# Eight-expert loop written out with one expert-number load per tile, and linear attention's q products and tail rearranged

## The chip, the core and the metric

The kernel runs on one core of a Trainium2 chip. The metric is device time in microseconds (us) for one execution. A core has TensorE (PE; its weight loads are shown as PEld), VectorE (DVE), ScalarE (ACT), GpSimd (POOL), and SyncE (SP), which here only issues transfers. Each engine works through its own list of instructions in order; semaphores order the engines among each other.

## What is computed

A chain of eight residual blocks on x of 2 x 1024 tokens with 256 features in fp32: x = x + block(layernorm(x)). The blocks are causal attention, a mixture of four experts (one for each token), a keyed sum, the four experts again, linear attention, a mixture of eight experts (two for each token, with a shared expert), causal attention, and the eight experts again. The change concerns linear attention and the two eight-expert blocks:

```python
# linear attention, 16 heads of 16; decay = exp(-pos / n)
Q = relu(x @ Wq.T + bq) * decay;  K = relu(x @ Wk.T + bk) * decay;  V = x @ Wv.T + bv
KV = einsum('bhnd,bhne->bhde', K, V);  Ksum = K.sum(axis=2)
Z = 1.0 / (einsum('bhnd,bhd->bhn', Q, Ksum)[..., None] + 1e-6)
out = (einsum('bhnd,bhde->bhne', Q, KV) * Z) @ Wo.T + bo

# eight experts, hidden 176, the two best of each token; shared expert with hidden 352
scores = softmax(x @ gate_w);  topk_w, topk_idx = top_k(scores, 2)
g = silu(x @ w_gate[e]) * (x @ w_up[e])
routed = sum over the two e of topk_w * (g @ w_down[e])
out = routed + silu(x @ sw_gate) * (x @ sw_up) @ sw_down
```

## The kernel before

The 2048 tokens are 16 tiles of 128, in four groups g of four tiles. The stages follow each other; each writes its instructions on every engine in a fixed order by hand, with semaphore waits. PSUM has eight banks of 512 fp32 columns.

**Eight experts (`TopTwo`).** Routing sorts the 4096 token copies by expert into 39 tiles of 128 rows; each tile belongs to one expert, whose number lies in `owner`. The matmuls read it into a register of TensorE's queue (`tile_owner`, `value_load`) and address the expert's weights with it. For a tile k POOL gathers its rows from DRAM (`gather`, L1418) into one of three buffers `y`; TensorE transposes them (`turn_y`, L1766), DVE copies the transposes (`set_y`, L1886), TensorE makes gate and up products (`up`, L1773), ACT the silu (L1841), DVE the product h (L1890), TensorE transposes h (`turn_h`, L1783), DVE copies it (L1899), TensorE multiplies down (`down`, L1791 and L1792), ACT copies the answer into one of three buffers `o` (`out`, L1847), and POOL scatters it to DRAM (`store`, L1422). TensorE, ACT and DVE run this by `every_tile`: three tiles written out, a loop of eleven rounds of three tiles, three tiles written out. POOL's list is written out for all 39 tiles: wait for `turn_y` of k, gather k+3, store k-2. A step of TensorE for k is `turn_y(k+2)`, `up(k+1)`, `turn_h(k)`, `down(k-1)`; `up` and `down` each load the expert number. Routing and the first group of the shared expert stand ahead of the loop, the other groups of the shared expert (L1747, L1758) behind it.

**Linear attention (`LinearAttention`).** The norm ahead of it (`LayerNorm`) adds the results of the experts on DVE (L1436), takes statistics, normalizes tile pairs (L287), and TensorE transposes the normalized tiles group by group (`turn`, L321); ACT copies the transposes to `yt` (L337). Then TensorE makes for each group two q products (L2152, banks 0 and 1; ACT's ReLU L2188) and four key and value products (L2160, banks 2 and 3), behind all groups the sums over tokens (L2169), and for each of the 16 tiles the product with the sums (L2178, bank t % 4). DVE takes each tile through four instructions: denominator (L2218), reciprocal (L2220), times decay (L2222), and product (L2224). The projection (`Project`) transposes the 16 results by groups (`turn`, L375; copies by ACT L405, and by DVE for one half of the first group, L411), multiplies (L387) into banks 0 to 3, and DVE adds to x (L417). `finished` lets the first group's `turn` go only when all 16 tiles are done.

The weights of linear attention are issued by SP (L2131) behind the loads of the experts' results.

Of the kernel before, what the change touches and what calls it, by code (L numbers as in the profile page):

```python
# [12 lines left out]
P = 128  # L13
# [9 lines left out]
RING = 3  # L23
GQ = 4
# [52 lines left out]
class Core:  # L77


    def __init__(self, nc, ctx):  # L80
# [21 lines left out]
        self.answers = nc.dram_tensor("answer_rows", [RING * P + 2 * NTOK, D], F32, kind="Internal").ap()  # L102
# [55 lines left out]
class Stage:  # L158
# [17 lines left out]
    def tile_done(self, dve, t): pass  # L176

# [51 lines left out]
class LayerNorm(Stage):  # L229
# [6 lines left out]
    def __init__(self, c, k, before):  # L236
# [11 lines left out]
        self.early_logits = None  # L248
# [83 lines left out]
    def scalar(self, act):  # L332
        c, k = self.c, self.k
        for g in range(NG):
            for f, done in enumerate((self.yt0, self.yt1)[0:2 if g < NG - 1 else 1]):
                act.wait_ge(self.turned, FT * (NG * k + g) + f + 1)
                act.activation(c.yt[:, f, 512 * g:512 * g + 512], self.bank(g, f)[:, :],  # L337
                               ACT.Copy).then_inc(done, 1)


class Project(Stage):
# [7 lines left out]
    def __init__(self, c, k, source, w, before):  # L349
        self.c, self.k, self.source, self.w, self.before = c, k, source, w, before  # L350
# [7 lines left out]
    def tensor(self, pe):  # L358
# [748 lines left out]
class Routing(Stage):  # L1107
# [12 lines left out]
    def __init__(self, c, kind, ln, experts, top, w, bias, const, carve, **more):  # L1120
# [46 lines left out]
        self.spare_rows = P if top == 1 else RING * P  # L1167
        if top == 2:
# [5 lines left out]
        ln.early_logits = self.multiply_logits  # L1174
# [3 lines left out]
            orders=e + (RING if top == 2 else 0), hits=1, before=1, owners=1, counters=4, stored=16 * NG, hot=4 * top, tile_hot=2 * top, scaled=top,  # L1178
# [32 lines left out]
    def gpsimd(self, pool):  # L1211
# [3 lines left out]
        if self.top == 2:  # L1215
            spare = self.spare.rearrange("p (i j) -> p i j", j=RING)
            for j in range(RING):
                pool.memset(spare[:, :, j:j + 1], float(P * j)).then_inc(self.orders.sem, 1)
# [169 lines left out]
    def set_rows(self, dve):  # L1388
# [6 lines left out]
        if self.top == 2:  # L1395
            dve.wait_ge(self.orders.sem, self.orders.at(self.e + RING))
            then(dve, dve.tensor_scalar(self.row_outf, rows[:, 0:tiles], float(RING - 1), float((RING - 1) * P), ALU.mult,
# [232 lines left out]
class TopTwo(Routing):  # L1630
# [6 lines left out]
    def __init__(self, c, ln, experts, weights, w, const, carve):  # L1637
# [3 lines left out]
        per_slot = 16 * (tiles // RING)  # L1641
        super().__init__(
            c, "top_two", ln, experts, 2, w, None, const, carve, y_in0=per_slot, y_in1=per_slot, y_in2=per_slot,
            y_turned=tiles, y_set=tiles, gu=tiles, silu=tiles, h_clear=RING, h_done=tiles, h_turned=tiles,
            ht_set=tiles, down=tiles, o_set=tiles, o_out0=per_slot, o_out1=per_slot, o_out2=per_slot, gathered0=32,
# [3 lines left out]
         self.h_turned, self.ht_set, self.down, self.o_set, o_out0, o_out1, o_out2, g0, g1, g2, g3, added1,  # L1649
# [872 lines left out]
```

## Time and profile before

| | us |
|---|---|
| median of 3 runs (2033.89 to 2037.41) | 2034.59 |
| the profiled execution | 2033.5 |
| its span, first to last instruction | 2031.4 |
| TensorE busy in the span | 1817.6 (89%) |
| VectorE busy | 1124.7 (55%) |
| ScalarE busy | 756.8 (37%) |
| GpSimd busy | 553.4 (27%) |
| share of TensorE in the chain of work that ended last | 73% |

The span is what the hardware profiler saw between the first and the last instruction. An engine's busy time leaves out register, branch and semaphore instructions; "issue" in a row means that an engine waited for nothing the profile shows. [...]

### The profile page before, as it was taken

How to read it: one execution, taken by the hardware profiler on the slowest of the kernel's cores; microseconds unless marked ns; L12 is line 12 of the kernel's file. 1: busy time of each engine (PE TensorE's matmuls, PEld its weight loads, DVE VectorE, ACT ScalarE, POOL GpSimd, SP SyncE). 2: the span in 40 equal slices, each digit the busy share in tenths (PEclk: the TensorE clock that was granted, in tenths of full speed). 3: DMA queues.
4: the chain of work that ended last, by engine and by line, in shares of the span. 5: the costliest groups of instructions: out<-in, count | busy, mean ns of one | idle time of the engine just before them, and what ended most of it. 6: DMA issues, size and time to landing. Idle time of an engine off the chain costs nothing.

```text
span 2031.4 us, 32807 instructions
## 1 busy us (share of the span) xinstructions
PE 1817.6 (89%) x10668; PEld 1014.0 (50%) x10673; DVE 1124.7 (55%) x2329; ACT 756.8 (37%) x1469; POOL 553.4 (27%) x950
## 2 busy tenths in 40 slices
PE   7799999998979997776999878898987999988988
PEld 4344444443446664464666536565553444455654
DVE  6688888886332222873222155733465888746334
ACT  3277777776411111112111110222132676741221
POOL 2322222222201111451111130256223222223650
PEclk9599999999789999878999979999996999998999
DMA  3311111114210002001000140122414122001223
GB/s 108 91 32 38 41 41 41 41 41 167 85 55 26 21 23 85 25 1 57 21 23 23 41 156 1 59 78 85 129 45 90 24 41 40 3 30 57 82 78 124
DMA packets 82063, 114.22 MB, mean 56 GB/s; under 512 B 17272, under 2 KB 61464, under 8 KB 81176
## 3 DMA queue, kind: packets, MB, share of 16 engines
q1 hardware_dynamic: 70808, 82.23, 14.0%
q0 software_dynamic: 11136, 30.42, 4.7%
q8 instruction: 72, 1.18, 0.2%
q14 instruction: 47, 0.39, 0.1%
HBM read 78.35 MB, written 33.69 MB: 55 GB/s over the span
## 4 chain that ended last, share of the span: by engine, by line
PE 73%; DVE 15%; issue 4%; DMA 3%; POOL 1%; ACT 1%; SPq 0%; another core or an unknown queue 0%; POOLq 0%; DVEq 0%; ACTq 0%
PE psum L1530 13%; PE psum L1057 10%; PE psum L1041 8%; PE psum L1551 6%; PE psum L1002 6%; DVE region_a L805 6%; PE psum L1773 5%; PE psum L1747 3%; PE psum L1791 2%; PE psum L1758 2%; PE psum L1792 2%; PE psum L1540 2%; PE psum L2160 1%; PE psum L931 1%; PE psum L1026 1%
## 5 line engine op out<-in xcount | busy, mean ns | idle before, releaser
L805 DVE TENSOR_REDUCE region_a<-psum 128x1 f32<-128x640 f32 (+7 forms) x576 | 528.2, 954 | 108.1 <-PE psum L1007 58.1
L909 ACT ACTIVATE region_w<-psum 128x512 f32<-128x512 f32 x864 | 465.6, 600 | 222.1 <-PE psum L1041 218.6
L1530 PE MATMUL psum<-region_w,region_a 128*128 x608 | 271.0, 599 | 1.4 <-DVE region_a L1611 1.2
L1057 PE MATMUL psum<-region_w,region_a 128*32 128x512 f32 (+3 forms) x2304 | 253.8, 514 | 1.0 <-POOL region_w L732 0.6
L732 POOL TENSOR_SCALAR_AFFINE_SELECT region_w<-region_w 128x512 f32<-128x512 f32 x192 | 121.8, 635 | 458.4 <-ACT region_w L909 454.1
L1422 POOL DMA_INDIRECT answer_rows<-region_a x116 | 114.5, 987 | 423.3 <-ACT region_a L1580 345.6
L1002 PE MATMUL psum<-region_a,y_norm 48*128 48x512 bf16 (+7 forms) x816 | 224.4, 351 | 5.0 <-DVE region_a L805 4.3
L1041 PE MATMUL psum<-y_norm,region_a 51*128 51x512 bf16 (+1 forms) x612 | 205.4, 399 | 6.1 <-DMA y_norm<-region_a 4.2
L1530 PEld LDWEIGHTS psum<-region_w,region_a 128*128 128x128 f32 x608 | 113.8, 192 | 132.0 <-issue 132.0
L1618 DVE TENSOR_TENSOR region_a<-psum,region_a 128x512 f32<-128x512 f32 x76 | 52.5, 691 | 214.9 <-PE psum L1530 214.9
L1418 POOL DMA_INDIRECT region_a<-token_rows,region_a x116 | 112.9, 973 | 146.4 <-DVE region_a L1394 86.7
L1551 PE MATMUL psum<-region_w,region_a 128*128 x608 | 137.7, 379 | 1.9 <-ACT region_a L1590 1.9
L1041 PEld LDWEIGHTS psum<-y_norm,region_a 51*128 51x128 bf16 (+1 forms) x612 | 51.0, 96 | 160.8 <-ACT region_w L909 108.6
L1773 PE MATMUL psum<-region_w,region_a 128*128 x312 | 114.2, 489 | 18.4 <-issue 17.2
L1551 PEld LDWEIGHTS psum<-region_w,region_a 128*128 128x128 f32 x608 | 112.7, 190 | 17.1 <-issue 3.3
L1585 ACT ACTIVATE region_a<-psum 128x512 f32<-128x512 f32 x76 | 45.4, 597 | 187.0 <-PE psum L1530 187.0
L1005 PE MATMUL psum<-region_a 64*128 64x128 bf16 x512 | 112.8, 226 | 0.0
L1007 PE MATMUL psum<-region_a,identb 64*128 64x64 bf16 x512 | 98.0, 194 | 0.0
L321 PE MATMUL psum<-identf,y_norm 128*128 128x128 f32 x256 | 47.5, 340 | 56.3 <-DVE y_norm L287 46.0
L1623 DVE COPY region_a<-psum 128x512 f32<-128x512 f32 x38 | 26.3, 692 | 128.0 <-PE psum L1540 128.0
L1747 PE MATMUL psum<-y_t,region_w 128*128 128x512 f32 (+1 forms) x192 | 85.7, 594 | 0.9 <-ACT region_a L1847 0.9
L1002 PEld LDWEIGHTS psum<-region_a,y_norm 48*128 48x128 bf16 (+1 forms) x816 | 65.5, 99 | 41.7 <-DVE region_a L805 21.7
(218 smaller groups left out, 2631.2 us busy)
## 6 DMA issues: line engine op xcount, KB each, us to landing
y_norm<-a_q SPq DMA_DIRECT2D x132, 64.0 KB
token_rows<-y_norm SPq DMA_DIRECT2D x16, 512.0 KB, 5.2
y_norm<-answer_rows SPq DMA_DIRECT2D x16, 512.0 KB, 6.0
y_norm<-b_q SPq DMA_DIRECT2D x36, 128.0 KB
region_w<-in_f_wg SPq DMA_DIRECT2D x1, 4096.0 KB, 13.3
region_w<-in_f_wu SPq DMA_DIRECT2D x1, 4096.0 KB, 13.5
region_w<-in_f_wd SPq DMA_DIRECT2D x1, 4096.0 KB, 14.8
region_w<-answer_rows SPq DMA_DIRECT2D x8, 512.0 KB, 7.9
```

Source lines behind the costliest of these rows:

```text
L732: pool.affine_select(p, p, pattern=[[0, GQ], [1, P]], channel_multiplier=-1, base=0, compare_op=ALU.is_ge, fill=0.0)\
L805: dve.tensor_reduce(dst, src, AX_X, ALU.max, negate=True).then_inc(self.ring_done.sem, 1)
L909: act.activation(self.p[col % P_RING][:, :, i % 4, :], c.bank[ST_BANKS[s % 3]].rearrange("p (h t) -> p h t", h=GQ), ACT.Exp, scale=self.sc ...
L1002: mm = pe.matmul(bank[:, 0:n], q, kp[lo_row:hi_row, lo:lo + n], start=True, stop=not diag, skip_group_check=True)
L1041: mm = pe.matmul(bank[:, :], self.kp[slot][0:self.srows, P * j:P * j + P], self.qp[slot][0:self.srows, :, P * i:P * i + P], start=True, st ...
L1057: mm = pe.matmul(c.bank[ACC_BANK][32 * h:32 * h + 32, P * lo:512], self.vp[slot][:, j, :], self.p[col % P_RING][:, h, lo:4, :], start=(j = ...
L1418: pool.indirect_dma_start(y, None, self.c.tokens[:, :], bass.IndirectOffsetOnAxis(ap=self.row_in[:, k:k + 1], axis=0)).then_inc(done.sem, 16)
L1422: pool.indirect_dma_start(self.c.answers[0:self.spare_rows + self.top * NTOK, :], bass.IndirectOffsetOnAxis(ap=self.row_out[:, k:k + 1], a ...
L1530: mm = pe.matmul(bank[:, :], self.yt[:, f, :], w[:, f, bass.ds(own * self.hidden + 512 * half, 512)], start=(f == 0), stop=(f == FT - 1))
L1551: mm = pe.matmul(c.bank[7][:, 0:D], self.ht[:, j, :], self.wd[:, bass.ds((own * (last + 1) + j) * D, D)], start=(j == 0), stop=(j == last))
L1747: mm = pe.matmul(c.bank[6 * (n % 2) + k][0:m, :], weight[:, f, P * j:P * j + m], c.yt[:, f, 512 * g:512 * g + 512], start=(f == 0), stop=( ...
L1773: mm = pe.matmul(self.gu_bank[j][:, 0:2 * self.hidden], self.yt[j][:, f, :], w.wgu[:, f, bass.ds(own * (2 * self.hidden), 2 * self.hidden) ...
```

## The change

In `TopTwo`, `every_tile` writes all 39 tiles out. The expert number is loaded once for each tile, behind `up` of the tile before it, and kept until `down`. There are five answer buffers instead of three, in the space of `ctx` behind the shared expert's buffers, and POOL stores three tiles behind instead of two. In linear attention, the q products of groups 0 and 1 stand ahead of the norm's transposes of groups 2 and 3, with their ReLUs behind ACT's copies of groups 1 and 2. The tail takes two tiles at a time: the denominator is the sum plus EPS / decay, which leaves out the multiplication by decay. The projection's first `turn` waits for its own four tiles; its first products wait for all 16.

TensorE's list inside the expert loop, before; L1446 is the load of the expert number, for `up` (L1773) and for `down` behind `turn_h` (L1783), and ISA and REGISTER_ALU are register instructions:

```order
L1446 ISA
L1446 TENSOR_LOAD region_a
L1446 ISA x2
L1771 REGISTER_ALU
L1773 ISA
L1773 MATMUL psum<-region_w,region_a 128x352
L1773 ISA
L1773 MATMUL psum<-region_w,region_a 128x352
L1779 REGISTER_ALU
L1783 MATMUL psum<-identf,region_a 128x128 x2
L1446 ISA
L1446 TENSOR_LOAD region_a
```

The same list now, one step; L1774 is `turn_y`, L1781 `up`, L1458 the load, L1792 `turn_h`, L1800 and L1801 `down`:

```order
L1774 MATMUL psum<-identf,region_a 128x128 x2
L1781 ISA
L1781 MATMUL psum<-region_w,region_a 128x352
L1781 ISA
L1781 MATMUL psum<-region_w,region_a 128x352
L1458 TENSOR_LOAD region_a
L1458 ISA x2
L1792 MATMUL psum<-identf,region_a 128x128 x2
L1800 ISA
L1800 MATMUL psum<-region_w,region_a 128x256
L1801 ISA
L1801 MATMUL psum<-region_w,region_a 128x256
```

One load stands in a step instead of two, behind the `up` matmuls instead of ahead of them, and none ahead of `down`.

TensorE's list from the norm into linear attention, before (L321 transposes, L2152 q products, L2160 key and value products):

```order
L321 MATMUL psum<-identf,y_norm 128x128 x32
L2152 MATMUL psum<-y_t,region_a 128x512 x4
L2160 MATMUL psum<-region_a,y_t 128x512 x8
L2152 MATMUL psum<-y_t,region_a 128x512 x4
L2160 MATMUL psum<-region_a,y_t 128x512 x8
```

The same place now (L323 transposes, L2179 q products, L2202 key and value products):

```order
L323 MATMUL psum<-identf,y_norm 128x128 x16
L2179 MATMUL psum<-y_t,region_a 128x512 x4
L323 MATMUL psum<-identf,y_norm 128x128 x8
L2179 MATMUL psum<-y_t,region_a 128x512 x4
L323 MATMUL psum<-identf,y_norm 128x128 x8
L2202 MATMUL psum<-region_a,y_t 128x512 x16
```

Two groups of q products moved between the transposes, and two groups of key and value products now follow each other.

DVE's list in the tail, before, two tiles:

```order
L2218 TENSOR_SCALAR region_a<-psum,region_a 128x16
L2220 RECIPROCAL region_a<-region_a 128x16
L2222 TENSOR_SCALAR region_a<-region_a 128x16
L2224 TENSOR_TENSOR ctx<-psum,region_a 128x256
L2218 TENSOR_SCALAR region_a<-psum,region_a 128x16
L2220 RECIPROCAL region_a<-region_a 128x16
L2222 TENSOR_SCALAR region_a<-region_a 128x16
L2224 TENSOR_TENSOR ctx<-psum,region_a 128x256
```

The same list now, four tiles:

```order
L2260 TENSOR_TENSOR region_a<-psum,region_a 128x32
L2263 RECIPROCAL region_a<-region_a 128x32
L2267 TENSOR_TENSOR ctx<-psum,region_a 128x256 x2
L2260 TENSOR_TENSOR region_a<-psum,region_a 128x32
L2263 RECIPROCAL region_a<-region_a 128x32
L2267 TENSOR_TENSOR ctx<-psum,region_a 128x256 x2
```

Two tiles have four instructions instead of eight.

The diff, cut to its core:

```diff
+O_RING = 5
...
 class LayerNorm
     def turn(self, pe, g):
-        if g == 3 and self.early_logits:
-            self.ready(pe, 1)
-            self.early_logits(pe, 0)
-            self.early_logits(pe, 1)
+        if self.early:
+            self.early.before_turn(pe, g)
...
     def scalar(self, act):
+            if self.early:
+                self.early.behind_copies(act, g)
...
 class Project
         def multiply(g):
             copied(0, g)
             copied(1, g)
+            if g == 0:
+                self.products_free(pe)
...
 class TopTwo
-    def every_tile(self, eng, step):
-        rounds = self.tiles // RING
-        for j in range(RING):
-            step(0, j, j, self.tiles - 1 - j)
-        with eng.Fori(1, rounds - 1) as i:
-            for j in range(RING):
-                step(i, j, i * RING + j, RING)
...
+    def every_tile(self, step):
+        for k in range(self.tiles):
+            step(k)
...
     def gpsimd(self, pool):
-            if k >= 2:
-                store(k - 2)
+            if k >= 3:
+                store(k - 3)
+        store(self.tiles - 3)
...
     def tensor(self, pe):
-        def up(i, j, k):
-            own = self.tile_owner(pe, k)
+        def up(k):
+            j = k % RING
...
-        def down(i, j, k):
-            own = self.tile_owner(pe, k)
+        def down(k):
+            j, own = k % RING, owner.pop(k)
...
+        def step(k):
+            if k + 2 < self.tiles:
+                turn_y(k + 2)
+            if k + 1 < self.tiles:
+                up(k + 1)
+            if k + 2 < self.tiles:
+                owner[k + 2] = self.tile_owner(pe, k + 2)
+            turn_h(k)
+            if k:
+                down(k - 1)
...
     def scalar(self, act):
+        def out(k):
+            j = k % O_RING
             act.wait_ge(self.down.sem, self.down.at(k + 1))
+            if k >= O_RING:
+                act.wait_ge(self.o_out[j].sem, self.o_out[j].at(16 * (k // O_RING)))
             act.activation(self.o[j], self.o_bank, ACT.Copy).then_inc(self.o_set.sem, 1)
...
 class LinearAttention
+    def before_turn(self, pe, g):
+        if g >= 2:
+            self.multiply_q(pe, g - 2)
+    def behind_copies(self, act, g):
+        if g in (1, 2):
+            self.relu_q(act, g - 1)
+    def multiply_q(self, pe, g):
+        c = self.c
+        if g == 0:
+            pe.wait_ge(self.w_in, self.W_IN)
+        self.ln.ready(pe, g)
...
     def vector(self, dve):
+        dve.reciprocal(self.eps, self.decay).then_inc(self.den_step, 1)
+        dve.wait_ge(self.den_step, 1)
+        dve.tensor_scalar(self.eps, self.eps, self.EPS, None, ALU.mult).then_inc(self.den_step, 1)
...
+        for n in range(NT // 2):
+            den, rden = self.den[n % 2], self.rden[n % 2]
+            both = c.psum[:, 2 * (n % 2):2 * (n % 2) + 2, 0:FT * (P + nh)].rearrange("p n (f e) -> p n f e", f=FT)
+            eps = over(self.eps[:, 2 * n % BT:2 * n % BT + 2], 2, FT * nh)
+            dve.wait_ge(self.outp, 2 * n + 2)
...
+            dve.tensor_tensor(den.rearrange("p n (f h) -> p n f h", f=FT), both[:, :, :, P:P + nh],
+                              eps.rearrange("p n (f h) -> p n f h", f=FT), ALU.add).then_inc(self.den_step, 1)
+            dve.reciprocal(rden, den).then_inc(self.den_step, 1)
+            for i in range(2):
+                t = 2 * n + i
+                dve.tensor_tensor(c.cx[:, D * t:D * t + D].rearrange("p (f h e) -> p f h e", f=FT, h=nh),
...
     def finished(self, pe, g):
-        pe.wait_ge(self.o_done, 4 * g + 4 if g else NT)
+        pe.wait_ge(self.o_done, 4 * g + 4)
+
+    def products_free(self, pe):
+        pe.wait_ge(self.o_done, NT)
```

## Rows read from the trace of the kernel before

**Rows 1.** Busy time by stage: stretch, length, engines' busy us, PEclk, DMA share, GB/s
```profile
1171.00:1188.00 17.00, 8.82 (x33) 6.02 (x34) 15.33 (x51) 3.55 (x7) 9.34 (x19) 0.50 0.27 87
...
1854.80:1976.90 122.10, 109.78 (x465) 73.19 (x465) 42.54 (x116) 27.35 (x78) 72.37 (x74) 0.99 0.25 79
```

**Rows 2.** The chain that ended last, three expert steps: start us, us, what
```profile
1380.67 0.27 issue
...
1383.87 0.58 issue
...
1390.36 1.45 PE psum L1773 x4
```

**Rows 3.** Register instructions, 1380 to 1382.5: count, ns min/median/max, first and last start
```profile
L1446 PEldq FUSED_REGOPS  x4: 46/106/151, 1380.0 to 1381.8; - x4
L1446 PEldq TENSOR_LOAD <-region_a x2: 300/302/303, 1380.1 to 1381.5; - x2
...
L1773 PEldq FUSED_REGOPS  x2: 46/46/46, 1380.8 to 1381.0; - x2
```

**Rows 4.** TensorE in order of time, expert loop: start us, us, instructions [idle before]
```profile
1322.02 1.35 PE L1773 MATMUL psum<-region_w,region_a 128*128 x4
...
1324.51 1.35 PE L1773 MATMUL psum<-region_w,region_a 128*128 x4
...
1429.86 1.36 PE L1773 MATMUL psum<-region_w,region_a 128*128 x4
...
1436.74 2.84 PE L1747 MATMUL psum<-y_t,region_w 128*128 128x512 f32 x6 [0.47 <-ACT region_a L1847]
```

**Rows 5.** POOL in order of time in the same loop
```profile
1323.97 0.97 POOL L1418 DMA_INDIRECT region_a<-token_rows,region_a  x1 [0.30 <-issue]
...
1326.54 0.97 POOL L1418 DMA_INDIRECT region_a<-token_rows,region_a  x1 [0.30 <-issue]
```

**Rows 6.** The gathers' line over the whole execution: ns min/median/max, and landing
```profile
L1418 POOL DMA_INDIRECT region_a<-token_rows,region_a x116: 941/970/1201, 573.1 to 1963.5; - x116
...
DMA to landing us min/median/max: 2.6/2.7/3.0
```

**Rows 7.** TensorE in order of time, the norm ahead of linear attention
```profile
1178.08 1.11 PE L321 MATMUL psum<-identf,y_norm 128*128 128x128 f32 x4 [1.17 <-DVE y_norm L287]
```

**Rows 8.** The line that loads linear attention's weights, its last load
```profile
L2131 SPq DMA_DIRECT2D region_a<-in_member x1: 428/428/428, 1170.1 to 1170.1; - x1
...
DMA to landing us min/median/max: 6.1/7.0/7.7
```

**Rows 9.** The chain that ended last, start of linear attention
```profile
1188.10 5.44 PE psum L2152 x8
1193.54 6.87 PE psum L2160 x16
1200.41 3.43 PE psum L2152 x8
```

**Rows 10.** DVE in order of time, tail of linear attention and the projection's copy
```profile
1239.17 0.23 DVE L2218 TENSOR_SCALAR region_a<-psum,region_a 128x16 f32<-128x16 f32 x1
1239.43 0.26 DVE L2220 RECIPROCAL region_a<-region_a 128x16 f32<-128x16 f32 x1
1239.72 0.24 DVE L2222 TENSOR_SCALAR region_a<-region_a 128x16 f32<-128x16 f32 x1
1239.99 0.42 DVE L2224 TENSOR_TENSOR ctx<-psum,region_a 128x256 f32<-128x256 f32 x1
...
1257.38 0.42 DVE L2224 TENSOR_TENSOR ctx<-psum,region_a 128x256 f32<-128x256 f32 x1
...
1259.93 0.69 DVE L411 COPY y_t<-psum 128x512 f32<-128x512 f32 x1 [2.13 <-PE psum L375]
```

**Rows 11.** TensorE in order of time, the same stretch
```profile
1241.72 0.70 PE L2178 MATMUL psum<-region_a,region_w 128*128 128x136 f32 x4 [0.46 <-DVE ctx L2224]
...
1261.32 4.79 PE L387 MATMUL psum<-region_a,y_t 128*128 128x256 f32 x16
```

More of the change, by code:

```diff
@@ L1166, in __init__ @@
         self.row_out = self.row_in
[L1167 removed]
+        self.spare_rows = P if top == 1 else O_RING * P
         if top == 2:
@@ L1641, in __init__ @@
         per_slot = 16 * (tiles // RING)
+        o_slots = {f"o_out{i}": 16 * len(range(i, tiles, O_RING)) for i in range(O_RING)}
         super().__init__(
@@ L1661, in __init__ @@
         self.sh = [r.take([512]) for _ in range(3)]
+        self.o = [r.take([D]) for _ in range(O_RING)]
         self.back = [c.yn, Carve(c.region["w"], weights.end).take([NT, D])]
@@ L1793, in down @@
                 .then_inc(self.down.sem, 1)
-        def step(i, j, k, left):
-            if left >= 2:
-                turn_y(*self.later(i, j, 2))
-            if left >= 1:
-                up(*self.later(i, j, 1))
-            turn_h(i, j, k)
-            if not (isinstance(k, int) and k == 0):
-                down(*self.later(i, j, -1))
+        def step(k):
[6 more added lines that the diff above has]
+            turn_h(k)
+            if k:
+                down(k - 1)
         assert w.shared_tiles == 3
@@ L1816, in tensor @@
         pe.wait_ge(self.s_added.sem, self.s_added.at(2))
-        for j in range(2):
-            turn_y(0, j, j)
-        up(0, 0, 0)
-        self.every_tile(pe, step)
-        down(self.tiles // RING - 1, RING - 1, self.tiles - 1)
+        for k in range(2):
+            turn_y(k)
+            owner[k] = self.tile_owner(pe, k)
+        up(0)
+        self.every_tile(step)
+        down(self.tiles - 1)
         pe.wait_ge(self.o_set.sem, self.o_set.at(self.tiles))
@@ L1859, in scalar @@
             self.scale_lanes(act, k)
-        silu(0, 0, 0)
-        self.every_tile(act, step)
-        out(self.tiles // RING - 1, RING - 1, self.tiles - 1)
+        silu(0)
+        self.every_tile(step)
+        out(self.tiles - 1)
         for n in range(m, 4 * m):
@@ L1891, in mul, with step @@
                               ALU.mult).then_inc(self.h_done.sem, 1)
-        def step(i, j, k, left):
-            if left >= 2:
-                set_y(*self.later(i, j, 2))
-            if left >= 1:
-                mul(*self.later(i, j, 1))
+        def step(k):
+            j = k % RING
+            if k + 2 < self.tiles:
+                set_y(k + 2)
+            if k + 1 < self.tiles:
+                mul(k + 1)
             dve.wait_ge(self.h_turned.sem, self.h_turned.at(k + 1))
@@ L1912, in vector @@
         dve.wait_ge(self.h_clear.sem, self.h_clear.at(RING))
-        for j in range(2):
-            set_y(0, j, j)
-        mul(0, 0, 0)
-        self.every_tile(dve, step)
+        for k in range(2):
+            set_y(k)
+        mul(0)
+        self.every_tile(step)
         pairs_behind = {5: 0, 6: 1, 7: 2, 8: 3, 10: 4, 11: 5}
```

147 lines of the change are left out of this document (76 added, 71 removed).

## The prediction

> **What bounds the kernel now.** I read the busy times by stage first, to see which of the edited places are limited by TensorE. Two are the expert loops of the two top-two stages: 122.10 us for the second, with TensorE busy 109.78 of it at a granted clock of 0.99 [rows 1]. The third is the linear attention with the norm ahead of it. In that norm, 1171 to 1188, TensorE is busy 8.82 of 17.00 us at a clock of 0.50 while DVE is busy 15.33 [rows 1]: DVE sets the pace and TensorE has room.
>
> In the loop I then read the chain of waits over three steps. One `up` begins behind a gap at 1380.67 + 0.27 = 1380.94, the third after it at 1390.36 [rows 2], so a step takes 9.42 / 3 = 3.14 us. The chain is TensorE all along, with gaps that read "issue", the largest here 0.58 us ahead of an `up` [rows 2]: TensorE has its data and waits for its own instruction queue. What sits there is the load of the expert number. Its first register instruction starts at 1380.0, the load at 1380.1 takes 300 ns, and the first register instruction of the matmul starts at 1380.8 [rows 3]: 0.8 us of queue, twice in a step, because `up` and `down` each load the number. Where the queue was ahead, a whole step took 1324.51 - 1322.02 = 2.49 us [rows 4]. So 0.65 us of each step is queue, at most 0.33 for each load, if the branch and the register arithmetic cost nothing beside them.
>
> POOL is the next limit: a gather and a store together take 1326.54 - 1323.97 = 2.57 us when neither waits [rows 5]. So the loop can fall from 3.14 to about 2.57, not below.
>
> **The change part by part. The loops.** Written out, a step loses one load, the register arithmetic and a third of a branch. The load that stays moves behind the two `up` matmuls. Their four records take 1.35 us [rows 4] and cover 0.8 us of queue, as long as the queue runs ahead of the array. I cost that load at nothing; if the cover fails it costs up to 0.33 a step. POOL's program has no loop before or after, so its instructions keep their price. It stores three tiles behind the gather now instead of two, so a store finds its answer ready, and the gather behind it starts earlier. Five answer buffers keep ACT's copy from waiting for a scatter: with 2.57 us a tile the buffer comes round after 12.9 us. A gather lands 2.7 us after its issue [rows 6] and has about three steps, 7.7 us, to do so. I see no wait added for DVE or ACT, whose queues lose their loops too.
>
> The sum for the first loop: the `up` at 1324.51 is the fifth of 39 [rows 4], so 34 follow.
> - By TensorE: 1324.51 + 34 x 2.49 = 1409.2 for the last `up`.
> - By POOL: the gather at 1323.97 is the seventh [rows 5]; with the later store the eighth stands there, and 31 remain to the last. 1323.97 + 31 x 2.57 + 2.7 for landing + one step of 2.49 = 1408.8.
>
> The two limits nearly meet, and two such limits jostle each other, so I take 1410. From the last `up` to the shared experts it is 1436.74 - 1429.86 = 6.88 us [rows 4], made of waits between engines, which I keep. The loop then ends at 1416.9 instead of 1436.74: 19.8 us. The second has the same span within 1 us, so both give 39.6 us.
>
> **The q products.** Two of four groups move between the transposes of the norm. TensorE reaches the first when the second group's transposes end, 1178.08 + 1.11 = 1179.2 [rows 7]. It then waits for the stage's weights: the last load is issued at 1170.1 and takes at the least 6.1, at the most 7.7 us to land [rows 8], so 1176.2 to 1177.8, with 1.4 us in hand. If they came later, the transposes queued behind would wait, and with them ACT's copies, but DVE's norm would not. In the kernel before, the first q group took 5.44 us and the second 3.43 [rows 9]. I take 5.44 for the first, since it again starts at the low clock, and 3.43 for the second. Between them and after come eight transposes each; four take 1.11 us at the low clock [rows 7], so eight take 1.1 at the high one. 1179.2 + 5.44 + 1.1 + 3.43 + 1.1 = 1190.3. The key and value products then start at 1190.3 instead of 1193.54, and the 3.43 us of the second q group between them are gone [rows 9]: 3.2 + 3.4 = 6.6 us. ACT's two new ReLUs stand between copies whose transposes come later in TensorE's own order, so they delay nothing.
>
> [...]
>
> **The tail.** Per tile DVE does four instructions, at 1239.17, 1239.43, 1239.72 and 1239.99; the last of sixteen such tiles has its product at 1257.38 [rows 10], so a tile takes (1257.38 - 1239.99) / 15 = 1.16 us and the product itself 1.16 - 0.82 = 0.34. A pair is now 0.26 + 0.29 + 2 x 0.34 = 1.23, eight pairs 9.8 instead of 18.5 us: 8.7 saved. I take 8.5, since two of the instructions are twice as wide. TensorE must deliver two tiles in 1.23 us; four records take 0.70 when they start from a wait [rows 11], and the second tile's start when a pair ends. That fits; at 1.40 a pair it would cost 1.4 us in all. The two small new instructions for eps over decay lie ahead of the key products' first result, beside TensorE.
>
> Then `turn` of the projection no longer waits for all sixteen tiles. Before, DVE's last product ended at 1257.38 + 0.42, its own copy came at 1259.93 [rows 10], and the first projection product at 1261.32 [rows 11]: 3.5 us. Now the transposes lie beside the last pair, and what remains is DVE's copy, 0.69 us, and its hand-over: 0.9. Saved: 2.6.
>
> Linear attention in all: 6.6 + 8.5 + 2.6 = 17.7 us. **Sum:** 39.6 + 17.7 = 57.3. The profiled execution took 2033.5 (its span 2031.4 and 2.1 around it), 1.1 under the median 2034.59. 2033.5 - 57.3 = 1976.2, so a median of about **1977**.
>
> **The rivals.**
> 1. The load that stays is not covered. For it: in the loop before, the queue does fall behind the array. Against it: one load less per step gives the queue back 0.8 us where 0.65 were missing. Price: 2.49 + 0.33 = 2.82 a step, 34 x 0.33 = 11.2 a loop, the gain 8.6: 2033.5 - 17.2 - 17.7 + 1.1 = 2000.
> 2. POOL's issues stretch when the other engines crowd beside it. A gather's issue takes 0.97 in the median and 1.20 at its longest [rows 6]. If all took 1.20, the pair would be 2.80, 31 x 0.23 = 7.1 later in each loop: 1991. Against it: beside a DVE that was busy a third of the loop the median stays at 0.97. [...]
> 3. The q products gain nothing, since the clock stays at 0.50 under them: 2 x 6.86 for products and 2 x 2.2 for transposes end at 1197.3 instead of 1190.3. That eats the 6.6 whole: 1984. Against it: the rise seen in the same products [rows 9].
> 4. Slower: the load behind `up` runs only once those matmuls have left the array. The queue's 0.8 us then stand bare in every step, with 0.2 to restart: 3.49 a step, 0.35 x 34 = 11.9 more in each loop, less the 17.7: 2033.5 + 23.8 - 17.7 + 1.1 = 2041. It decides from 0.92 us a step (0.65 + 17.7 / 68). Against it: the 0.8 us of queue from 1380.0 [rows 3] left a gap of only 0.27 in the chain [rows 2], so the load ran while earlier matmuls were in the array.
>
> **How the numbers follow.** Forecast 0.64, rivals 0.12, 0.10, 0.10 and 0.03; 0.01 for something that cancels by chance. The forecast's own ends are 1966 (tighter hand-overs at the loop's end and a warmer projection) and 1985. The range of eight in ten takes in rivals 2 and 3 and part of the way to rival 1: 1966 to 1996. A measurement here tells 0.2% (4 us) from no change. Only rival 4 is slower: faster 0.96, same 0.01, slower 0.03.
>
> **What would show it.** Steps of `up` 2.5 to 2.6 us apart, POOL nearly without idle in the loop and "issue" gone ahead of `up`; key products starting near 1190; tail pairs 1.25 us apart; the first projection product within 1 us of DVE's last. Steps near 2.8 with "issue" behind the load would mean rival 1, POOL issues above 1.1 us rival 2. I am wrong if a step stays at 3.1: then the wait was never the loads.

## The result, and the profile of the kernel after

The changed kernel takes 2007.83 us (median of 4 runs, 2005.97 to 2012.86) against 2034.24 for the kernel before on the same chip (4 runs): 0.9867 of its time, with a 95% interval of 0.9848 to 0.9885. It is faster by 26.4 us (1.3%), clear of the noise, where 57.3 us were forecast; the time is outside the range. The profiled execution took 2007.0, its span is 2005.2.

Linear attention gave about 19 us, a little more than the 17.7 forecast. The loops gave 5 each instead of 20. TensorE in order of time in the first loop (start us, us, instructions [idle before]); L1781 is `up`, L1792 `turn_h`, L1752 the shared expert behind the loop:

```profile
1296.64 2.71 PE L1781 MATMUL psum<-region_w,region_a 128*128 x4
...
1325.92 1.35 PE L1781 MATMUL psum<-region_w,region_a 128*128 x4
...
1328.40 1.35 PE L1781 MATMUL psum<-region_w,region_a 128*128 x4
...
1330.89 1.35 PE L1781 MATMUL psum<-region_w,region_a 128*128 x4
1334.23 0.41 PE L1792 MATMUL psum<-identf,region_a 128*128 128x128 f32 x2 [1.99 <-DVE region_a L1916]
...
1335.66 1.35 PE L1781 MATMUL psum<-region_w,region_a 128*128 x4
...
1407.78 1.35 PE L1781 MATMUL psum<-region_w,region_a 128*128 x4
...
1414.29 1.98 PE L1752 MATMUL psum<-y_t,region_w 128*128 128x512 f32 x4 [0.47 <-ACT ctx L1861]
```

The first `up` of the loop before, in the same view, and then the page's line for `up` in both loops, before and after (busy us, mean ns | idle ahead of it). The count is one of records: the two matmuls of `up` for each of 2 x 39 tiles, 156 in the program, stand in both traces as 312, the two transposes of `turn_y` as 156 (L1766 before, L1774 after):

```profile
1313.76 2.71 PE L1773 MATMUL psum<-region_w,region_a 128*128 x4
```
```profile
L1773 PE MATMUL psum<-region_w,region_a 128*128 x312 | 114.2, 489 | 18.4 <-issue 17.2
```
```profile
L1781 PE MATMUL psum<-region_w,region_a 128*128 x312 | 111.5, 482 | 0.3 <-DVE region_a L1901 0.2
```

Most steps are as forecast: 1328.40 - 1325.92 = 2.48 and then 2.49 us, against 3.14 before [rows 2], and the 17.2 us of "issue" ahead of `up` are gone. But the next step takes 4.77, and such a step comes about every fourth time. From the first `up` to the last it is 1407.78 - 1296.64 = 111.1 us, 2.92 for each of 38 steps; to the shared experts it is 117.7, against 1436.74 - 1313.76 = 123.0 before (the end in [rows 4]). The second loop takes 117.5 instead of 122.1 [rows 1].

The long step in the same view for ACT (L1854 is the silu, L1861 the copy of the answer) and, last row, DVE (L1916, the copy of h):

```profile
1328.39 0.39 ACT L1861 ACTIVATE ctx<-psum 128x256 f32<-128x256 f32 x1 [0.77 <-PE psum L1801]
1332.25 0.32 ACT L1854 ACTIVATE region_a<-psum 128x176 f32<-128x176 f32 x1 [3.48 <-PE psum L1781]
1333.72 0.38 ACT L1861 ACTIVATE ctx<-psum 128x256 f32<-128x256 f32 x1 [1.15 <-remote]
```
```profile
1333.66 0.43 DVE L1916 COPY region_a<-psum 128x256 f32<-128x256 f32 x1 [0.71 <-remote]
```

ACT's silu at 1332.25 needs the `up` that began at 1328.40 and ended at 1329.75 by TensorE's row. It starts 2.5 us after that, though ACT had nothing else to do and the silu waits for nothing but its `up`. "Remote" is the page's word for a releaser that it can't name: at 1333.66 and 1333.72 DVE and ACT start within 0.1 us of each other, on transposes and products of TensorE that had ended 3.7 and 2.9 us earlier. TensorE's signals come late here. Those of the others don't: `turn_h` at 1334.23 follows DVE's end at 1334.09. The lateness stands in no row of TensorE's, where `up` has its usual 1.35 us, only in the idle time of those who wait, such as ACT's 3.48 us ahead of the silu. Whether the matmul itself ended late or only its signal came late, no row tells; this text calls both a late signal.

POOL over the same stretch; L1434 is the store, L1430 the gather:

```profile
1322.27 0.99 POOL L1434 DMA_INDIRECT answer_rows<-ctx,region_a  x1 [1.63 <-ACT ctx L1861]
1323.56 0.97 POOL L1430 DMA_INDIRECT region_a<-token_rows,region_a  x1 [0.30 <-issue]
...
1331.28 0.97 POOL L1430 DMA_INDIRECT region_a<-token_rows,region_a  x1 [0.30 <-issue]
1334.38 0.99 POOL L1434 DMA_INDIRECT answer_rows<-ctx,region_a  x1 [2.12 <-ACT ctx L1861]
```

From 1322.27 to 1332.25 POOL issues eight indirect transfers without a pause, at the durations of before [rows 5]. ACT's late start at 1332.25 falls on the end of the eighth. That is a hint, not a proof; the experiments had to show which of the things in the loop makes the signals late.

### The profile page after: what moved, and what is told of

The parts are those of the page before. It is cut to its first block, busy times and chain, and to the rows that moved or that the text cites. A ratio compares the mean times of both kernels' runs of the same rounds, so it can differ in the third digit from the quotient of the medians.

```text
span 2005.2 us, 31961 instructions
## 1 busy us (share of the span) xinstructions
PE 1801.9 (90%) x10672; PEld 1012.1 (50%) x10673; DVE 1121.3 (56%) x2299; ACT 755.6 (38%) x1469; POOL 555.1 (28%) x954
## 4 chain that ended last, share of the span: by engine, by line
PE 70%; DVE 16%; issue 4%; DMA 3%; another core or an unknown queue 2%; POOL 1%; ACT 1%; SPq 0%; POOLq 0%; DVEq 0%; ACTq 0%
PE psum L1542 13%; PE psum L1064 9%; PE psum L1048 7%; DVE region_a L812 7%; PE psum L1563 7%; PE psum L1009 6%; PE psum L1781 4%; PE psum L1752 3%; PE psum L1763 2%; PE psum L1800 2%; PE psum L1552 2%; PE psum L1801 1%; PE psum L938 1%; PE psum L1033 1%
## 5 line engine op out<-in xcount | busy, mean ns | idle before, releaser
L1430 POOL DMA_INDIRECT region_a<-token_rows,region_a x116 | 113.1, 975 | 147.5 <-DVE region_a L1406 86.8
L1434 POOL DMA_INDIRECT answer_rows<-region_a x38 | 37.6, 990 | 345.5 <-ACT region_a L1592 345.5
L1781 PE MATMUL psum<-region_w,region_a 128*128 x312 | 111.5, 482 | 0.3 <-DVE region_a L1901 0.2
L1434 POOL DMA_INDIRECT answer_rows<-ctx,region_a x78 | 77.2, 990 | 66.8 <-ACT ctx L1861 49.1
L323 PE MATMUL psum<-identf,y_norm 128*128 128x128 f32 x256 | 44.7, 326 | 52.4 <-DVE y_norm L291 42.2
L1752 PE MATMUL psum<-y_t,region_w 128*128 128x512 f32 (+1 forms) x192 | 85.7, 594 | 0.9 <-ACT ctx L1861 0.9
```

Of the source, the lines that this page charges most:

```text
L1430: pool.indirect_dma_start(y, None, self.c.tokens[:, :], bass.IndirectOffsetOnAxis(ap=self.row_in[:, k:k + 1], axis=0)).then_inc(done.sem, 16)
L1434: pool.indirect_dma_start(self.c.answers[0:self.spare_rows + self.top * NTOK, :], bass.IndirectOffsetOnAxis(ap=self.row_out[:, k:k + 1], a ...
L1752: mm = pe.matmul(c.bank[6 * (n % 2) + k][0:m, :], weight[:, f, P * j:P * j + m], c.yt[:, f, 512 * g:512 * g + 512], start=(f == 0), stop=( ...
L1781: mm = pe.matmul(self.gu_bank[j][:, 0:2 * self.hidden], self.yt[j][:, f, :], w.wgu[:, f, bass.ds(owner[k] * (2 * self.hidden), 2 * self.hi ...
```

## The experiments

All of them are compared by the time from the first `up` to the last in the first loop: 116.1 us before, 111.1 after. (The expectations call this 37 steps; it is 38.) A loop of 2.49 us steps throughout takes 94.0. Traces of one and the same loop code differ by some 2 us (that of the kernel before took 116.1 us here and 113.9 in lin_only), so a smaller difference between two traces tells nothing.

### Which of three things in the loop: the load, the place in the program, or the stores

const_owner, the register load and the address arithmetic away:

```
-                owner[k + 2] = self.tile_owner(pe, k + 2)
+                owner[k + 2] = (k + 2) // 5
```

> The changed kernel, but the expert number of tile k is the constant k // 5: nothing is loaded into a register and no address is computed in the expert loops (the answers use other experts' weights, the work is the same). In the changed kernel a free step is 2.49 us, but every fourth step or so TensorE's signals to ACT and DVE come 1 to 2.8 us late, and first up to shared experts takes 117.6 us. Theory 1, the register load makes TensorE's signals late: no late signals, 39 steps of 2.49, about 103 us a loop, 1978 in all. Theory 2, the lateness comes at fixed distances in TensorE's instruction stream (about 130 recorded instructions from one to the next): with 25 or 26 instead of 33 a step it comes every fifth step instead of every fourth, some 3 us a loop, 2001. Theory 3, the gathers and stores on POOL's queue cause it: unchanged, 2007.

Measured: 2006.43 us, 109.5 from first to last `up`. Long steps remain (one of them, 1342.23 to 1346.31, in the timeline of its `up`s):

```profile
1342.23 1.45 PE L1781 MATMUL psum<-region_w,region_a 128*128 128x352 f32 x4
1346.31 1.35 PE L1781 MATMUL psum<-region_w,region_a 128*128 128x352 f32 x4
1348.80 1.35 PE L1781 MATMUL psum<-region_w,region_a 128*128 128x352 f32 x4
```

Theory 1 falls; the 1.7 us less than in after lie within the difference between traces.

pe_loop0 is the changed kernel, but TensorE alone keeps its loop, with one load a tile in a register of its own, at a chosen place of the program; before_slot only moves TensorE's loop in the kernel before. If the place in the program made the signals late, as theory 2 has it, the loop in another place would change that:

```
+        with c.nc.Fori(1, rounds - 1, engines=[pe.engine], head_slot={pe.engine: 0}) as i:
+            for j in range(RING):
+                step(i, j, i * RING + j, RING)
...
+        at = {eng.engine: 0} if eng is self.c.nc.tensor else None
+        with self.c.nc.Fori(1, rounds - 1, engines=[eng.engine], head_slot=at) as i:
```

> [...] Theory 2 (place in the instruction stream): no late signals inside the loop, steps of 2.5 to 2.6, a loop of 103 to 107 us, 1978 to 1986. Theory 1 (register load) and theory 3 (POOL's queue): late signals as in the changed kernel, 113 to 118 a loop, 2000 to 2008.

> [...] In the kernel before, one signal in each round of three tiles is about 1 us late. Theory 2: that lateness goes, a round takes 8.4 instead of 9.4 us, 11 rounds, 2 loops: 2034 - 22 = 2012. Theories 1 and 3: 2034, as before.

Measured: pe_loop0 2012.58 (4 runs, 2007.27 to 2014.28), 115.2 in the loop; before_slot 1.0015 of before (1.0004 to 1.0026). Theory 2 falls. And writing TensorE's loop out was worth little by itself: with it kept, the kernel takes 0.9874 of before (0.9848 to 0.99), which can't be told from 0.9867, though the loop in its one trace is 4 us longer than in after.

no_store, the indirect stores away:

```
-            self.scatter(pool, k, self.o[k % O_RING], self.o_out[k % O_RING])
+            pass
```

> The changed kernel without the 39 stores of answers in each expert loop (what is read back afterwards are token rows, as many bytes). Theory 3, the queue's stores make TensorE's signals late: steps of 2.49 throughout, about 103 us instead of 117.6 from the first up to the shared experts, 1978 in all. Theories 1 and 2 (register load, place in the instruction stream): the loops stay at 115 to 118 us, 2003 to 2007.

Measured: 1975.24 us, 94.0 in the loop, and every step 2.49:

```profile
1341.41 1.35 PE L1781 MATMUL psum<-region_w,region_a 128*128 x4
1343.90 1.35 PE L1781 MATMUL psum<-region_w,region_a 128*128 x4
1346.38 1.35 PE L1781 MATMUL psum<-region_w,region_a 128*128 x4
```

Theory 3 holds: the stores cost the loop 17 us. The kernel without stores comes near the 1977 us that I had forecast for the change with them.

### What of a store counts

narrow_store writes 16 numbers a row instead of 256; half_rows sends 64 of the 128 rows; no_gather keeps the stores and drops the gathers behind the third; no_store_incs has no stores, but SP raises a semaphore as often. Theory A is that the completions of the transfers crowd TensorE's signals (the kernel waits for a count of 16 for each transfer), theory B that the bytes do, theory C that POOL's indirect issues do:

```
-            self.scatter(pool, k, self.o[k % O_RING], self.o_out[k % O_RING])
+            pool.indirect_dma_start(narrow[0:self.spare_rows + self.top * NTOK, :], ...
+                                    self.o[k % O_RING][:, 0:16], None)
...
+                                    bass.IndirectOffsetOnAxis(ap=self.row_out[0:64, k:k + 1], axis=0),
+                                    self.o[k % O_RING][0:64, :], None)
...
-                self.gather(pool, k + RING, self.y[k % RING], self.y_in[k % RING])
...
+            for i in range(16):
+                sp.sem_inc(self.o_out[0].sem, 1)
```

> The changed kernel, but each store of an answer writes 64 bytes a row instead of 1024 (what is read back afterwards are token rows). The same number of issues by POOL, of rows and of completions, a sixteenth of the bytes. Without the stores the 37 steps from the second up on took 94.0 us, with them 111.1. [...] Theory B, the bytes: 94 to 96. Theory C, the number of indirect issues on POOL: stays near 111.

> The changed kernel, but each store sends 64 of the 128 rows (what is read back afterwards are token rows). If the number of rows counts, a pair needs 1.5 issues' worth, 0.75 x 2.96 = 2.22 us, under the free step: 94 to 97 us for the 37 steps. If the issue as such counts, whatever its rows: 110 to 111 us.

> The changed kernel with its stores, but without the gathers behind the first three (the later tiles use the rows that lie in the buffers). Theory A, completions: half as many, as without the stores, so 94 to 96 us for the 37 steps. Theory B, bytes of the stores: stays near 111. Theory C, indirect issues on POOL: half as many, 94 to 96.

> The kernel without stores, but for each tile SP raises a semaphore that nobody waits for 16 times, as the completions of a store do. Theory A, semaphore updates crowd TensorE's signals: late signals come back, 103 to 111 us for the 37 steps. Theories B and C: 94, no late signals.

Measured, first to last `up`: narrow_store 111.4 us, half_rows 110.6, no_gather 94.0, no_store_incs 94.3. Neither bytes nor rows count (theory B falls), nor do semaphore updates alone (theory A). Gathers alone do no harm, stores alone neither: in the loop it takes both, two indirect issues a tile. Groups of POOL's instructions in half_rows (line, count | busy us, mean ns | idle):

```profile
L1430 POOL DMA_INDIRECT region_a<-token_rows,region_a x31 | 29.8, 961 | 11.8 <-issue 9.7 <-PE psum L1776 2.1
L1701 POOL DMA_INDIRECT answer_rows<-ctx,region_a x28 | 25.6, 912 | 24.2 <-ACT ctx L1863 18.5 <-issue 5.8
```

Half the rows take 912 ns to issue instead of 990, and POOL still waits for ACT: it is not POOL that is short of time.

### Is it that POOL is busy, or that it issues

plain_store stores by plain transfers from SP's queue, pool_plain by plain transfers from POOL's; pool_busy and pool_busy4 store nothing and let POOL fill local memory two or four times a tile instead:

```
+            sp.dma_start(self.c.answers[at:at + P, :], self.o[k % O_RING])
...
+            pool.dma_start(self.c.answers[at:at + P, :], self.o[k % O_RING])
...
+            for i in range(4 * k, 4 * k + 4):
+                pool.memset(self.idle, 0.0)
```

> The changed kernel, but the answers are stored to rows in order by plain transfers on SP's queue, 128 KB each, with 16 completions each, and POOL issues the gathers alone (what is read back afterwards are token rows). Theory A, completions: late signals stay, 105 to 111 us. Theory B, bytes: near 111. Theory C, indirect issues on POOL: 94 to 96.

> The kernel without stores, but where a store stood POOL fills 128 x 256 numbers in its local memory twice, 2 x 0.57 us, about the time of a store's issue, with no transfer behind it (what is read back afterwards are token rows). Theory C-busy, a POOL that is busy all the time delays TensorE's signals: late signals, about 110 us for the 37 steps. Theory C-issue, the descriptors of the indirect transfers do it: 94 us, no late signals.

> As pool_busy, with four fills of 0.31 us for each tile instead of two: 4 x 0.31 and a gather of 0.95 are 2.2 us of POOL for each tile of 2.49, more than the 1.96 of a gather and a store. If a busy POOL delays TensorE's signals: late signals, 105 to 111 us from the first to the last up. If the indirect transfers do it: 94 us.

> The changed kernel, but POOL stores the answers with plain transfers to rows in order, on its own queue, as many as before (what is read back afterwards are token rows). If any transfer that POOL issues counts: 105 to 111 us from the first to the last up, as with indirect stores. If only indirect ones do: 94 us, as with plain stores on SP's queue.

Measured: plain_store 94.0, pool_busy 93.9, pool_busy4 94.7, pool_plain 94.1. Busy times from 1300 to 1390 (length, busy us of PE, PEld, DVE, ACT, POOL, then TensorE's granted clock as a share of full speed, DMA share, GB/s), after, pool_busy4, pool_plain, in this order:

```profile
1300.00:1390.00 90.00, 81.36 (x371) 58.28 (x370) 34.95 (x95) 20.88 (x61) 58.44 (x60) 0.98 0.27 87
```
```profile
1300.00:1390.00 90.00, 89.81 (x431) 66.87 (x431) 40.06 (x110) 25.06 (x72) 75.19 (x170) 1.00 0.18 52
```
```profile
1300.00:1390.00 90.00, 90.00 (x428) 66.79 (x427) 39.06 (x107) 24.57 (x70) 54.12 (x69) 0.99 0.32 102
```

In pool_busy4 POOL is busy 75.19 of 90 us, more than the 58.44 of after, and TensorE isn't held up: a busy POOL is harmless. (pool_busy told less: its fills took 0.31 us. The 0.57 was the mean of a group of fills of several shapes.) In pool_plain POOL issues as many transfers as in after and they move more bytes in the time, 102 against 87 GB/s: harmless too. no_store had also taken away ACT's wait for a landed store; no_gather, whose stores are indirect, keeps that wait at 94.0, so it isn't the cause. What is left is the indirect issue, two of them for each tile. A plain issue is shorter as well (587 ns in the mean in pool_plain, 990 for an indirect store in after), so whether its kind or its length counts stays open.

step_282 makes TensorE's step longer than POOL's pair, so that POOL has time to pause:

```
-            for f in range(FT):
+            for f in (0, 1, 0, 1):
```

> The changed kernel, but TensorE does more in each step: the two transposes of the gathered rows twice, and one of the two of h twice, 0.33 us more, so that a free step is 2.82 us, longer than POOL's pair of 2.57. Theory C1, POOL's two indirect issues a tile need about 2.96 us in something that they share with TensorE's signals, however they are spaced: the 37 steps stay at 110 to 111 us. Theory C2, it is that POOL issues without a pause, and any pause clears it: no late signals, steps of 2.82, 104 to 105 us, so a longer step makes a shorter loop.

Measured: 111.4 in the loop. Here are three of its `up`s:

```profile
1331.65 1.35 PE L1781 MATMUL psum<-region_w,region_a 128*128 x4
...
1334.47 1.35 PE L1781 MATMUL psum<-region_w,region_a 128*128 x4
...
1338.04 1.35 PE L1781 MATMUL psum<-region_w,region_a 128*128 x4
```

Free steps of 2.82 and then one of 3.57: 0.33 us more work in each step, and the loop is as long as without it. Theory C1 holds: the pair of indirect issues needs some 2.92 us, 1.46 for each on average. A pause doesn't clear it: in this run's trace POOL paused 0.53 to 0.55 us ahead of each of four stores, from 1305.97 to 1314.42, and behind them ACT's copy at 1317.57 still came 1.0 us after its `down` had ended (1316.53). A shorter step of TensorE only collects the difference into a rarer, longer stall.

### The two parts alone

lin_only has the linear attention of after and, with the class `TopTwo` of before, its expert loops (too long to print). before_no_store takes the stores out of the kernel before, as no_store does:

```
-            self.scatter(pool, k, self.o[k % RING], self.o_out[k % RING])
+            pass
```

> The kernel before with the linear attention's part of the change alone (q products inside the norm, tail by pairs, projection's transposes ahead); the expert loops are those of the kernel before. By the traces of before and after the first up of the first loop came 17.1 us earlier though the stage ahead of the linear attention ended 1.9 us later: 19 us from this part, 2034 - 19 = 2015. By the prediction 17.7 us: 2016.

> The kernel before without the 39 stores of answers in each expert loop (what is read back afterwards are token rows). It still loads the expert number twice a tile. If the loads in TensorE's queue made its step 3.14 us instead of 2.49, as the prediction has it, the steps stay near 3.1 and 37 of them take 115 us. If it was POOL's two indirect issues a tile, the steps fall to 2.5 to 2.7 and 37 of them take 94 to 100 us.

Measured: lin_only 2013.15 (4 runs), 0.991 of before (0.9891 to 0.993), 19.6 us less. before_no_store 2004.63, 98.6 us in the loop; its `up`s:

```profile
1361.83 1.45 PE L1773 MATMUL psum<-region_w,region_a 128*128 x4
...
1364.45 1.45 PE L1773 MATMUL psum<-region_w,region_a 128*128 x4
...
1367.03 1.35 PE L1773 MATMUL psum<-region_w,region_a 128*128 x4
```

Its steps are 2.6 us with both loads and the loop in them (98.6 / 38 = 2.59). So of the 0.65 us between 3.14 and 2.49 the loads and the loop made 0.10 by themselves. The other 0.55 go with the stores: they were the indirect issues, in the kernel before already.

### A version that goes around it

If one indirect issue a tile is harmless, the stores have to go elsewhere. sorted_answers writes each tile's answers in the order of the tiles, by a plain transfer on SP's queue, and gathers them back by token behind the loop, 32 indirect gathers beside the shared experts. sorted_paced lets these go three or four at a time, as DVE's products of the shared experts come out, and moves the final sums one step back:

```
+            sp.dma_start(self.c.answers[P * k:P * k + P, :], self.o[k % O_RING])
+            pool.indirect_dma_start(self.back[k][:, t, :], None, self.c.answers[0:self.tiles * P, :],
+                                    bass.IndirectOffsetOnAxis(ap=self.place_in[k][:, t:t + 1], axis=0))
...
+                pool.wait_ge(self.s_mul.sem, self.s_mul.at(muls))
```

> The changed kernel, but each tile's answers are stored in the order of the tiles by a plain transfer on SP's queue, and POOL gathers them back by token behind the loop, 32 indirect gathers beside the shared experts and the next norm instead of 39 indirect stores in the loop. Theory C (two indirect issues a tile make TensorE's signals late): 37 steps take 94 us instead of 111, 17 us for each of two loops, 2007 - 34 = 1973, if the gathers, 32 x 1.29 = 41 us of POOL, stay hidden beside the shared experts (some 49 us); 1973 to 1993 if the gathers make signals late there. If it fails: 2000 or more.

> As the kernel that gathers the answers back behind the loop, but the 32 gathers are let go three or four at a time, as DVE's products of the shared experts come out, one per 1.3 to 1.7 us instead of one per 1.25, and the final sums wait a step longer for them. There, back to back, they held TensorE's signals for 24 us at the end and took the whole gain of the loops. If issues at this pace are carried: the 34 us of the loops less 3 to 8 us for each late end, 1980 to 1990. If they still crowd: 1995 to 2010.

Measured: sorted_answers 2009.17 (4 runs), no better than after, though its loops take 94.3 and 94.1 us. The gain is lost behind the loops. The last stage, POOL, ACT (L1852, the shared silu) and TensorE:

```profile
1933.79 0.95 POOL L1696 DMA_INDIRECT y_norm<-answer_rows,region_a  x1 [17.61 <-issue]
...
1972.62 0.95 POOL L1696 DMA_INDIRECT region_w<-answer_rows,region_a  x1 [0.30 <-issue]
```
```profile
1977.29 0.60 ACT L1852 ACTIVATE ctx<-psum 128x512 f32<-128x512 f32 x1 [29.88 <-remote]
```
```profile
1948.34 3.60 PE L1755 MATMUL psum<-y_t,region_w 128*128 128x512 f32 x8
...
1953.50 3.60 PE L1755 MATMUL psum<-y_t,region_w 128*96 128x512 f32 x8
1980.20 3.75 PE L1766 MATMUL psum<-region_w,ctx 128*128 128x256 f32 x8 [23.10 <-DVE x_res L1899]
```

The 32 indirect issues start 1.25 us apart. The first signals still pass; then ACT waits 29.88 us, at its end for products of 1948.34 that by their row had ended 25.4 us earlier, and TensorE, waiting in turn for DVE behind ACT, 23.10. ACT goes on 3.7 us after the last issue ended, 43.5 us after the first began, 1.36 us for each. It is the lateness of the loop again, made by gathers alone; in the loop POOL runs out of answers to store when the signals stop, and here nothing stops it.

sorted_paced takes 1982.80 (4 runs, 1979.23 to 1985.01), 0.9743 of before (0.9722 to 0.9764), and beats both kernels. It changes two things, the pace and the place of the sums, and I didn't run them apart. At the same place it has:

```profile
1962.27 3.60 PE L1763 MATMUL psum<-y_t,region_w 128*96 128x512 f32 x8
1966.80 5.42 PE L1774 MATMUL psum<-region_w,ctx 128*128 128x256 f32 x24 [0.93 <-DVE x_res L1907]
```

No idle time above 1 us is left on TensorE there. The gathers are 1.50 us apart in the mean (the first of the 32 at 1927.08, the last at 1973.57). The lateness isn't quite gone. Behind the first loop, 14 gathers in a row, 1.25 to 1.36 us apart, end with a signal 3.2 us late: TensorE's products end at 1419.40, ACT's silu starts at 1422.64:

```profile
1415.80 3.60 PE L1763 MATMUL psum<-y_t,region_w 128*128 128x512 f32 x8
```
```profile
1422.64 0.60 ACT L1860 ACTIVATE ctx<-psum 128x512 f32<-128x512 f32 x1 [7.77 <-remote]
```

Of the 33.7 us that the two loops give (111.1 to 94.3, 111.0 to 94.1), routing, the later sums and norms, and the end keep 11.8 in the profiled executions: the span is 1983.3 instead of 2005.2.

It made no difference whether SP or POOL issued the plain stores (94.0 us in the loop from SP, 94.1 from POOL); only the indirect stores beside the gathers took it to 111.1.

## Why the prediction was wrong, step by step

- **The steps' floor was right.** 2.49 us a step by TensorE was read from [rows 4]; no_store has it in every step and the loop is 22.4 us shorter than before (first `up` 1299.42, shared experts 1399.99) where I had forecast 19.8. The load that stays costs nothing that shows, as said: no_store has it in each of its steps of 2.49.
- **The step that failed:** "So 0.65 us of each step is queue". The gaps ahead of `up` and the 0.8 us of register instructions (PEldq in the trace) [rows 2, rows 3] were real, but over both loops the gaps that read "issue" ahead of `up` made 17.2 us, 0.22 for each of 78 steps; the rest of the 0.65 was put down to the queue without a row. And even the gaps told who came last, not what is gained by taking that away. before_no_store shows the share of the loads and the loop: 0.10. The other 0.55 went with the stores, as late signals and what follows from them. Once in each round ACT's copy of an answer came about 1 us late, for a `down` that had ended at 1386.97, and DVE's copy of the gathered rows came late with it, for transposes that had ended at 1387.19:

```profile
1388.10 0.39 ACT L1847 ACTIVATE region_a<-psum 128x256 f32<-128x256 f32 x1 [1.85 <-PE psum L1792]
```
```profile
1388.06 0.43 DVE L1886 COPY region_a<-psum 128x256 f32<-128x256 f32 x1 [1.11 <-PE psum L1766]
```

DVE's copy needs no answer buffer, so the three buffers of before, which the change made five, weren't what held ACT. TensorE waits for these copies: both end at 1388.49, its `down` starts at 1388.74, and the load for the `up` at 1390.36 comes at 1389.5; the gap of 0.28 us ahead of this `up` reads "issue".
- **"POOL is the next limit: ... 2.57"** named the right engine and the wrong resource. POOL's issues kept their 0.97 and 0.99 us and POOL waited 23.2 us for ACT in the loop. What is limited is the number of indirect transfers, 2.92 us for two, in something that holds TensorE's signals back and that no row of POOL shows. From the first `up` to the last I had 1410 - 1313.76 = 96.2 us; it took 111.1.
- **Rival 1** (a load that shows, 2000) came near the measured time by luck, for a reason that wasn't there. **Rival 2** (POOL's issues stretch, 1991) had the right neighbours: the issues crowd, but they delay others instead of growing longer. I had no rival in which a transfer delays an engine that doesn't use it. (In rival 4, 0.65 + 17.7 / 68 is 0.91 and not 0.92; nothing hangs on it. Its 0.2 us to restart was my estimate, and no run shows it: no_store, with the load behind `up`, has steps of 2.49.)
- **The q products: 6.6 forecast, 7.3 measured.** The chain of waits of after (start us, us, what):

```profile
1181.19 4.73 PE psum L2179 x8
...
1186.79 3.44 PE psum L2179 x8
...
1191.10 5.17 PE psum L2202 x12
...
1225.96 7.14 PE psum L2211 x64
```

The first group took 4.73 where 5.44 was forecast, the second 3.44 as forecast. The stage ahead ended 2.0 us later than in the run before, so key products at 1191.10 are 1.2 ahead of the forecast 1190.3. The sums start at 1225.96, before at 1231.31 (row below): 5.4, and 7.3 with those 2.0. The shorter first group is the difference to 6.6. The granted clock in the trace of after was 0.50 from 1178 to 1181, 0.73 from 1181 to 1186 and 1.00 from 1186 to 1191; eight transposes of 1185.76 took 1.04 us, where four had taken 1.11 at 1180.08. So the clock rose under the moved products, and rival 3, in which it stays at 0.50, didn't happen.

```profile
1231.31 7.16 PE psum L2169 x64
```

- **The tail: 8.5 forecast, 8.3 measured; the hand-over: 2.6 forecast, 2.8 measured.** DVE, and behind it TensorE:

```profile
1242.35 0.76 DVE L2267 TENSOR_TENSOR ctx<-psum,region_a 128x256 f32<-128x256 f32 x2
...
1243.62 0.76 DVE L2267 TENSOR_TENSOR ctx<-psum,region_a 128x256 f32<-128x256 f32 x2
1244.30 0.68 DVE L418 COPY y_t<-psum 128x512 f32<-128x512 f32 x1
```
```profile
1245.08 1.10 PE L394 MATMUL psum<-region_a,y_t 128*128 128x256 f32 x4 [0.52 <-DVE y_t L418]
```

A pair takes 1.28 us in the mean of eight (1.23 forecast); the first projection product comes 0.7 us after DVE's last product, not 3.5 [rows 10, rows 11].
- **The sum.** Linear attention 18 to 19.6 (17.7 forecast), loops 9.9 (39.6 forecast): the term of the loops was too large by 30, and that is nearly the whole miss of 31.

## What to carry to other kernels

Before a gain is booked to a gap, leave out the work of its neighbours, one at a time, and see whether the gap stays: before_no_store, which keeps both loads, would have shown in one run that they were worth 0.10 us a step and the stores 0.55. Where an engine waits for a matmul that by its row has long ended, look at what POOL issues at that time: in this kernel two indirect transfers per 2.92 us were carried, and more held TensorE's signals back; one of the two can go as a plain transfer in sorted order, and the gathers behind it have to be spread: back to back they took the whole gain; spread to 1.50 us apart in the mean, and with the sums moved, most of it stayed.

## What the hardware showed that I had not expected

- In these runs TensorE's signals to ACT and DVE came late where POOL had issued indirect transfers one behind the other. What was carried is 1.46 us for each in the loop of after and 1.36 for each of the 32 behind the loop of sorted_answers, both estimates from the times above. No sharp limit follows: before has 116.1 / 38 / 2 = 1.53 us for each in the mean, in rows of six (one from 1379.35 to 1386.75, 0.30 us between its issues), and behind that row ACT and DVE came about 1 us late, at 1388.10 and 1388.06. It takes a while to build up: in the loop of after ACT came late at the end of eight issues in a row, and in sorted_paced the signals passed until 14 in a row had gone out, and the next came 3.2 us late. Their rows and bytes don't matter (half the rows 110.6, a sixteenth of the bytes 111.4 us, against 111.1), and plain transfers from the same queue do no harm (94.1).
- The signals of DVE and ACT came on time where I looked (1334.23 and 1334.38 in after). TensorE waited for no gather in the loop of after between 1300 and 1405; when the transfers landed there, the trace doesn't tell.
- What the transfers and TensorE's signals share stays open; no row shows it, and no run here was made that could tell. Every run was recorded by the profiler, so none shows whether it is the same unrecorded.
